# A wait for ScalarE's first ACTIVATE ahead of two of its DMA issues, in a two-layer cross-attention kernel

## The reference

```python
x = x + xattn0(layernorm(x), ctx, ctx, mask)   # 32 query heads, 8 key/value heads of 128, rope, tanh cap
x = x + lora_moe(layernorm(x))                 # 4 experts of rank 16, top 2
x = x + xattn1(layernorm(x), ctx)              # 16 query heads, 4 key/value heads of 96, keys: ctx and x
x = x + dense_lora(layernorm(x))               # x W' + bias + sum of 16 low-rank updates
```

## Time and profile before

| what | us |
|---|---|
| median of 3 runs | 832.24 (831.8 to 833.33) |
| the profiled execution's own time | 831.91 |
| its span | 829.7 |
| PE busy | 825.7 |
| DVE busy | 548.5 |
| ACT busy | 369.6 |
| POOL busy | 361.4 |

### The profile page before, as it was taken

How to read it: one execution, slowest core, us unless ns; L and a number is a source line. 1 busy time by engine, 2 the same in 40 slices (tenths; PEclk the granted TensorE clock), 3 DMA queues, 4 the chain that set the end, 5 groups by cost and what they waited for, 6 DMA issues and landing times.

```text
span 829.7 us, 11973 instructions
## 1 busy us (share of the span) xinstructions
PE 825.7 (100%) x4382; PEld 687.6 (83%) x4382; DVE 548.5 (66%) x1091; ACT 369.6 (45%) x920; POOL 361.4 (44%) x279
## 2 busy tenths in 40 slices
PE   9999999999999999999999999999999999999998
PEld 8888888877787877877877788898988888888887
DVE  6866856767776564747767746464366667677894
ACT  6443123124203124122223142567797877777762
POOL 4677445546637324533645340112232432366442
DMA  8122211311403202110311312011010200300002
GB/s 310 53 65 76 77 52 49 92 52 53 133 7 103 64 1 78 38 52 13 103 51 40 92 50 82 15 38 51 14 39 26 56 28 20 128 14 1 2 1 102
DMA packets 25786, 48.12 MB, mean 58 GB/s; under 512 B 4608, under 2 KB 5888, under 8 KB 25600
## 3 DMA queue, kind: packets, MB, share of 16 engines
q1 hardware_dynamic: 25296, 46.70, 18.9%
q10 hardware_dynamic: 432, 0.66, 0.2%
HBM read 45.12 MB, written 2.23 MB: 57 GB/s over the span
## 4 chain that ended last, share of the span: by engine, by line
PE 99%; DMA 1%; DVE 0%; SPq 0%; ACT 0%; issue 0%; DVEq 0%
PE PB L1417 23%; PE PB L1418 23%; PE PB L1419 23%; PE PB L1633 8%; PE PB L1564 4%; PE PB L1547 4%; PE PB L1424 4%; PE PB L1648 3%; PE PB L1461 2%; PE PB L1459 2%; PE PB L1456 2%; PE PB L1585 1%; DMA arena<-in_ctxT 1%; PE PB L1599 0%; PE PB L1486 0%; PE PB L1478 0%
## 5 line engine op out<-in xcount | busy, mean ns | idle before, releaser
L915 POOL TENSOR_TENSOR qb<-qb,arena 128x512 f32<-128x512 f32 x64 | 83.7, 1310 | 151.0 <-DVE arena L1262 151.0
L1173 DVE TENSOR_TENSOR xs<-xs,PB 128x512 f32<-128x512 f32 x111 | 75.6, 686 | 79.1 <-PE PB L1419 70.3
L992 ACT ACTIVATE Oh<-PB 96x128 fp32r<-96x128 f32 (+2 forms) x236 | 79.4, 360 | 66.4 <-PE PB L1564 47.3
L1417 PE MATMUL PB<-WOh,Oh 128*128 128x512 f32 x242 | 94.5, 390 | 0.0
L1418 PE MATMUL PB<-WOl,Oh 128*128 128x512 f32 x242 | 94.2, 389 | 0.0
L1419 PE MATMUL PB<-WOh,Ol 128*128 128x512 f32 x242 | 94.2, 389 | 0.0
L992 ACT ACTIVATE WOh<-stage 128x512 fp32r<-128x512 f32 (+1 forms) x32 | 19.2, 619 | 132.6 <-PE PB L1419 132.6
L892 POOL TENSOR_TENSOR WOl<-stage,WOh 128x512 fp32r<-128x512 f32 (+1 forms) x32 | 40.6, 1284 | 83.4 <-ACT WOh L992 63.6
L892 POOL TENSOR_TENSOR WQl<-stage,WQh 128x512 fp32r<-128x512 f32 x38 | 48.9, 1291 | 61.6 <-ACT WQh L992 52.1
L1417 PE MATMUL PB<-xTh,WQh 128*128 128x512 f32 x188 | 74.8, 398 | 0.0
L1418 PE MATMUL PB<-xTl,WQh 128*128 128x512 f32 x188 | 73.3, 390 | 0.0
(11 more groups left out here) (294 smaller groups left out, 2171.0 us busy)
## 6 DMA issues: line engine op xcount, KB each, us to landing
stage<-in_wq SPq DMA_DIRECT2D x44, 256.0 KB, 2.8
stage<-in_wo SPq DMA_DIRECT2D x44, 256.0 KB, 2.6
arena<-recs SPq DMA_DIRECT2D x32, 256.0 KB, 3.9
stage<-in_wk SPq DMA_DIRECT2D x12, 256.0 KB, 2.7
xs<-in_x SPq DMA_DIRECT2D x8, 256.0 KB, 6.7
arena<-in_ctxT SPq DMA_DIRECT2D x7, 256.0 KB, 6.3
out<-xs SPq DMA_DIRECT2D x7, 256.0 KB, 2.0
stage<-in_wvq SPq DMA_DIRECT2D x4, 256.0 KB, 3.7
```

Of the source, the lines that this page charges most:

```text
L915: e.tensor_tensor(dst, dst, tmp, ALU.add).then_inc(s_radd)
L992: return e.activation(dst, src, ACT.Copy)
L1173: e.tensor_tensor(xs[:, i, :], xs[:, i, :], PB[b][:, :], ALU.add).then_inc(free[b])
L1417: e.matmul(dst, Ah, Bh, start=(k == 0), stop=False)
```

## The change

Ahead of the issue of context quarter 1, ACT waits until s_fun is 1, which its own first ACTIVATE raises when it ends. The issue of the value half (L999) follows in ACT's order, so it comes after the wait too. Nothing else is changed.

```diff
                         act.wait_ge(s_one, 1)
                         move(sm[:, 0, 0, 0:1], pTb[:, 0, 0:1]).then_inc(s_fun)
                     if c == 1:
+
+                        act.wait_ge(s_fun, 1)
                         e.dma_start(cst[c][0], a["ctxT"][c * 128:(c + 1) * 128, 0:512]).then_inc(s_ldc[c], 16)
```

## The result

The changed kernel takes 834.97 us (median of 7 runs, 833.26 to 836.97) against 832.08 (7 runs, 831.76 to 833.33): 1.0036 times as long, 95% interval 1.0022 to 1.0051. That is 2.9 us slower, where 0.4 faster was forecast, and outside the range. The profiled execution took 834.41 us with a span of 832.3, 2.6 more than the 829.7 of the earlier trace rows.

A forecast was written before the change was run, and what follows sets the result against it. PE was taken to bound the kernel through the start of its first value matmul. Quarter 1 landing at 6.1 against a break-even of 6.50 gains 0.4: 832.24 - 0.4 = 831.8 us, range 831.0 to 833.4.

The forecast's parts named there:

- What bounds the kernel: PE, busy 825.7 of 829.7 us: some 4 us to win; moving the first value matmul (9.65) moves the end equally.
- The issue times: On ACT: quarter 1 from 1.22 to 2.70, value half from 1.63 to 3.11; key-weight rounding WKh 0.3 late, costing nothing.
- The break-even of 6.50 and the slope of 1: Start of the value matmuls: gain is 6.50 minus X, the time at which quarter 1 lands.
- The landing of quarter 1: Its DMA, issued at 2.70, was taken to need 3.4 us, landing at 6.1: gain 0.4 us.
- the lower bound of 2.8: Shortest transfer for quarter 1, from a 2.5 us wk half plus 0.32: landing 5.5, gain 1.0 us.
- the far bound of 8.4: Latest landing of quarter 1, with the value half's 5.7 us: a loss of 1.9 us.
- served in order of issue: Rival: quarter 1 stands behind all SP issued before 2.70, lands at 7.7, loss 1.2 us, 833.4; chance 0.23.
- The clock: Sign of being wrong: PE's granted clock, 1.00 at 2.4 GHz, falls while PE stands still longer; no size given.
- the first rival: Quarter 1's DMA served behind all SP's earlier issues: loss 1.2 us, 833.4 us; chance 0.23.
- Nothing that arrives for quarter 0 before 5.62 gains anything: PE's start: ten warm-up matmuls were said to last until the first key matmul at 5.62.
- The value half: Lands up to 2.3 us behind quarter 1, costing nothing with 0.2 to spare; as rival bound 832.2 us, chance 0.15.
- Further on: Layer norm: last DVE step ends at 14.41, its ACT reader starts at 15.00, so PE 0.4 us earlier still fits.

The follow-up runs named there:

- e4: Changed kernel, but SP issues x tile 0 and all behind it only once quarter 1 has landed (from 7.15): 833.86 us, 1.0024 of the kernel before.
- e3: Changed kernel, but only quarter 1 waits for the ACTIVATE, the value half being issued ahead at 1.21: 836.65 us, 1.0052 of the kernel before.
- e12: Changed kernel, but SP's quarter 2 and all behind it, and ACT's value half, wait until quarter 1 has landed: 834.41 us, late by design.
- e6: Changed kernel, but SP issues x tile 0 and all behind it only from 4.26 on: 832.41 us, 1.0007 of the kernel before.
- e9: Changed kernel, but SP issues quarter 1 as its fourth, after quarters 0, 2, 3; value half still behind ACT's wait: 835.34 us, 1.0046.
- e7: Changed kernel, but SP too waits for the ACTIVATE before issuing quarter 2 and what follows: 834.38 us, 1.0028 of the kernel before.
- e8: Changed kernel, but SP issues all four quarters in order, ACT only the value half behind the wait: 832.83 us, 1.0011 of the kernel before.
- e2: Kernel before, with only the value half's issue waiting for the ACTIVATE, quarter 1 as it was: 831.9 us, 1.0000 of the kernel before.
- e0: The changed kernel run again as a base for the others: 834.63 us, 1.0031 of the kernel before.
- e1: Changed kernel with five filler matmuls on PE behind the three of quarter 0: 833.93 us, 1.0025 of the kernel before.
- e10: Kernel before, no DMA moved, but PE waits for ACT's third context quarter before its first key projection: 834.64 us, 1.0034.

## Why the prediction was wrong

**What bounds the kernel** was right: the end moved with the first value matmul (9.65 to 12.22 and 829.7 to 832.3; 11.26 and 831.4 with ten fillers; 9.39 and 829.4 with the value half late). In every profile but two the end follows it by 820.0 to 820.3; in e4 it is 820.6 and in e3, where the matmuls stayed slow beyond it, 821.0. Only the bound of 4 us was misread: the busy time of PE counts the 4.6 us of warm-up too.

**The issue times** were right: 2.69 and 3.06 for 2.70 and 3.11, WKh at 3.62 for 3.58, hidden as said: in the chain the ACTIVATE ends at 2.67 and the issue starts at 2.69. The signal came with no drain behind the table load.

**The break-even of 6.50 and the slope of 1** were right for data that come late: 1.43 and 1.53 by the rule, 1.6 measured between medians.

**The landing of quarter 1 was mis-sized, and this is the step that failed.** 3.4 us were taken; it took 5.24 in the profile and 5.2 to 6.4 in the changed kernel with or without fillers. The two prices it was taken between (3.15 and 3.8) came from issues at 0.7 and 1.2 us, with at most one block ahead. The rows at hand for an issue nearer to 2.7 were those of SP in the earlier trace rows, 5.7 for one at 2.1 and 5.8 for one at 2.56; the forecast didn't use them. The bare 2.94 of e12 shows that the lower bound of 2.8 was sound, and 8.65 and 9.1 that even the far bound of 8.4 was too low. Nor did quarter 1 get its share at once, as the forecast had it from the turns between the queues: by 7.93 the SP queue had landed four blocks behind its half of wk0, the ACT queue one. The rival *served in order of issue* gave 7.7 and 833.4, one block less (e6) 7.1: near 7.93 and 7.10. That is in part luck. The same sum put x tile 0 at 7.1, 0.6 ahead of quarter 1, and it landed at 7.87, 0.06 ahead. In e9 the value half overtook quarter 1, e7 has two blocks ahead and lands at 7.52, and e9, with one block less than the changed kernel, at 8.41. So what fixes the landing time, order or sharing, stays open.

**The clock was left out of the sum.** It was named as what would make the prediction wrong, but without a price or a chance. It costs 1.1 us between medians here, on top of the 1.6 of late data; the first rival alone, 1.2, would have stayed within 0.2%. This also is why the chance of slower, 0.07, was far too low: it was set by one term alone.

**"Nothing that arrives for quarter 0 before 5.62 gains anything"** was wrong. The first key matmul can start behind the warm-up at 5.1 (5.3 in other runs); what had held it to 5.62 was quarter 0, which landed at 4.83. PE starts 0.8 behind that landing in each start where it comes at 4.5 or later (4.50 and 5.30 in e8, 4.78 and 5.57 in e9, 5.13 and 5.93 in e2). So the stop became longer at its front too: quarter 0 came earlier, PE was done with it at 6.2 instead of 6.8, and stood until 8.64.

**The value half** was no bound: it landed at 9.24, and its rounding was ready behind the late quarters well before 12.22. **Further on** nothing outran PE; it was later than all of them.

## What to carry to other kernels

While the transfers of a start are queued at the full rate, price an issue that is made later by the rows of issues at that later time, on whichever queue they stand, not by those of the first issues (the 5.8 us of x tile 0 would have given 8.5 here, between the 7.93 and the 9.1 measured); and delay the transfer that is needed last, not one in the middle of a chain. Here the quarters behind it landed early and lay unused, since ACT takes them in order; rounding them in the order in which they land was not tried. A wait of PE has two prices: how late it makes the work behind it (1.6 us here, of a stop of 2.4 to 2.7), and matmuls at half speed behind it (1.1 us more). Ten filler matmuls in the gap took the second away: their 11 runs all read a clock of 1.000 and lie within 1.2 us.

## What the runs showed of the hardware

In seven profiles PE stood still after it had reached the higher level and went on with matmuls 0.43 apart instead of 0.23, for some 3 to 6 us from its restart or soon behind it: stops of 2.40 (changed kernel), 2.66 (e0), 2.33 (e9), 1.86 (e3), 1.85 (e12), 1.58 (e6) and 1.43 us (e4). A stop of 2.04 in e1, one of 1.34 in e7 and the first of e3, 1.29, were not followed by slow matmuls. So the length of the stop doesn't settle it; what else does was not found. In e10 a stop of 2.12 came ahead of the rise, and the rise came only at 13.50.

Not settled is what holds a block up in company. In the profile of e7 the stretch 4 to 5 us moves only 117 GB/s, with five blocks issued and not yet landed, and the last columns of this row show it (clock, DMA share, GB/s):

```profile
4.00:5.00 1.00, 1.00 (x7) 1.00 (x7) 0.60 (x1) 0.79 (x2) 0.00 (x0) 1.00 0.35 117
```

A stretch at 117 instead of 399 moves 0.28 MB less, about one block, which is 0.7 us at that rate (an estimate). Weaker lulls stand in other starts too (236 in the kernel before, 260 in the changed one, in the same stretch, against 399 to 408 from 7 us on). In e1, whose DMA issues are those of the changed kernel, the lull is one microsecond later and deeper, and quarter 1 lands at 9.1 instead of 7.93:

```profile
5.00:6.00 1.00, 1.00 (x5) 0.90 (x5) 0.68 (x2) 0.00 (x0) 0.00 (x0) 1.00 0.56 111
```

So the lull changes from run to run of the same issues, and with it part of the landing times in the table, each of which is from one run. No run here told what it is.
